# A two-layer kernel gets its tokens already transposed: the first norm moves into the weights and into the residual

## The reference, cut to what matters

```python
def _layernorm(x, axis=-1, eps=1e-05):
    m = jnp.mean(x, axis=axis, keepdims=True)
    v = jnp.var(x, axis=axis, keepdims=True)
    return (x - m) / jnp.sqrt(v + eps)
...
        w_masked = weight * elem_mask.astype(weight.dtype)     # blocks of 32 x 32, kept where the mask's sum is > 0
        out = jnp.einsum('bsk,nk->bsn', data, w_masked)
...
        logits = x @ W_gate + b_gate
        _, top_idx = jax.lax.top_k(logits, TOP_K)               # 2 of 8 experts
        y_all = jax.nn.relu(jnp.einsum('bsd,edh->bseh', x, W_e) + b_e)
        y = jnp.take_along_axis(y_all, top_idx[..., None], axis=2)
        return y.mean(axis=2)
    x = L0_attn_data                                            # 4 x 512 tokens of 1024 features, fp32
    x = x + _L0_attn_ref(_layernorm(x, axis=-1), L0_attn_weight, L0_attn_mask)
    x = x + _L0_ffn_ref(_layernorm(x, axis=-1), L0_ffn_W_gate, L0_ffn_b_gate, L0_ffn_W_e, L0_ffn_b_e)
```

## Time and profile before

| | |
|---|---|
| median of 3 runs | 734.63 us (734.1 to 734.97) |
| the profiled execution's own time | 734.0 us |
| its span, first to last instruction | 732.3 us |
| TensorE busy | 708.0 us, 97% |
| VectorE (DVE) busy | 332.2 us, 45% |
| ScalarE (ACT) busy | 238.9 us, 33% |
| GpSimd (POOL) busy | 290.5 us, 40% |
| mean granted TensorE clock | 0.996 |

### The profile page before, as it was taken

How to read it: one execution, slowest core, us unless ns; L and a number is a source line. 1 busy time by engine, 2 the same in 40 slices (tenths; PEclk the granted TensorE clock), 3 DMA queues, 4 the chain that set the end, 5 groups by cost and what they waited for, 6 DMA issues and landing times.

```text
span 732.3 us, 11399 instructions
## 1 busy us (share of the span) xinstructions
PE 708.0 (97%) x3655; PEld 579.1 (79%) x3655; DVE 332.2 (45%) x667; ACT 238.9 (33%) x316; POOL 290.5 (40%) x302
## 2 busy tenths in 40 slices
PE   3999999999999999999999999999999999999994
PEld 2468888888777878888888888888888888888883
DVE  4756777778899665635254261062342540000000
ACT  2231311311532232433342324333332323333320
POOL 5612112112453315563545445363544445353430
PEclk9999999999999999999999999999999999999998
DMA  8723443447563437868669486487686674331313
GB/s 318 286 86 116 166 159 136 172 146 288 208 224 115 145 144 195 243 156 259 154 173 245 107 235 162 91 213 218 132 256 157 174 197 81 66 59 29 58 30 57
DMA packets 34502, 118.22 MB, mean 161 GB/s; under 512 B 5776, under 2 KB 5776, under 8 KB 34448
## 3 DMA queue, kind: packets, MB, share of 16 engines
q1 hardware_dynamic: 22032, 80.23, 30.3%
q0 software_dynamic: 11232, 37.23, 25.2%
q10 hardware_dynamic: 1184, 0.04, 0.1%
HBM read 83.40 MB, written 37.75 MB: 165 GB/s over the span
## 4 chain that ended last, share of the span: by engine, by line
PE 91%; DVE 5%; issue 2%; DMA 1%; ACT 0%; POOLq 0%; SPq 0%; DVEq 0%
PE psO L316 78%; PE psT L420 5%; PE psT L351 2%; PE psG L455 2%; PE psT L343 1%; PE psO L382 1%; DMA xb<-L_attn_data 1%; PE psS L382 1%; DVE row_hot L739 1%; DVE st L654 1%; PE psT L438 1%; DVE pos_i L730 1%; DVE xr L681 1%; DVE blk_hot L737 0%; PE psG L330 0%
## 5 line engine op out<-in xcount | busy, mean ns | idle before, releaser
L316 PE MATMUL psO<-slots,xT 128*128 (+1 forms) x1872 | 436.0, 392 | 0.0
L316 PEld LDWEIGHTS psO<-slots,xT 128*128 128x128 f32 x1872 | 348.3, 188 | 70.6
L316 PE MATMUL psO<-wT,xT 128*128 128x512 f32 x768 | 184.1, 395 | 0.0
L316 PEld LDWEIGHTS psO<-wT,xT 128*128 128x128 f32 x768 | 141.5, 188 | 29.8 <-issue 0.9
L1055 POOL DMA_INDIRECT rows_out<-xb,tok_of x37 | 62.8, 1697 | 222.5 <-ACT xb L622 216.3
L807 DVE CAST slots<-raw 128x1024 fp32r<-128x1024 f32 x56 | 57.1, 1020 | 192.5 <-PE psO L316 109.0
L622 ACT ACTIVATE xb<-psO 128x512 f32<-128x512 f32 x78 | 46.7, 599 | 253.7 <-PE psO L316 253.7
L1049 POOL TENSOR_TENSOR xT<-x2T,xT 128x1024 fp32r<-128x1024 f32 x38 | 99.7, 2624 | 18.5 <-ACT x2T L601 18.1
L809 DVE TENSOR_TENSOR slots<-raw,slots 128x1024 fp32r<-128x1024 f32 x56 | 72.8, 1299 | 1.9
L533 ACT ACTIVATE xT<-psT 128x1024 fp32r<-128x1024 f32 x17 | 17.5, 1027 | 147.1 <-PE psT L351 136.6
L564 ACT ACTIVATE psO<-bias_slot 128x512 f32 (+1 forms) x78 | 47.0, 602 | 36.3 <-ACT xb L622 18.6
(11 more groups left out here) (160 smaller groups left out, 467.7 us busy)
## 6 DMA issues: line engine op xcount, KB each, us to landing
raw<-L_ffn_W_e SPq DMA_DIRECT2D x56, 512.0 KB, 5.2
xb<-L_attn_data SPq DMA_DIRECT2D x16, 512.0 KB, 3.4
xr<-L_attn_data SPq DMA_DIRECT2D x16, 512.0 KB, 4.1
rows_out<-xr SPq DMA_DIRECT2D x16, 512.0 KB, 2.7
x_rows<-x SPq DMA_DIRECT2D x16, 512.0 KB, 2.9
mask_stage<-L_attn_mask SPq DMA_DIRECT2D x8, 512.0 KB, 11.6
w_stage<-L_attn_weight SPq DMA_DIRECT2D x8, 512.0 KB, 12.3
bias_slot<-L_ffn_b_e SPq DMA_DIRECT2D x8, 512.0 KB
```

Of the source, the lines that this page charges most:

```text
L316: last = eng.matmul(psum, xT[:, p, a, kt, :], moving(b, kt), start=(i == 0 and kt == 0 and not seeded), stop=(i == len(PASSES) - 1 and kt ...
```

## The change

The host also hands over the tokens with each 128x128 square transposed (`data_t`), so `xb` holds raw transposed tokens, and `transpose_x`, `norm1` and the matmuls and ACT passes that they cost go. ACT and DVE read the two parts from `xb` in SBUF instead of from PSUM. The mean of a token is taken off by taking the row mean off each row of the masked weight (`centre`, on ACT; the mean comes from a summing ACT pass for even r, from a summing DVE multiply for odd r, so POOL multiplies only even r). 1/std multiplies the product in the residual. `stats1` reads `xr` instead of `xb`, and stands one block ahead at the end of a step instead of two blocks ahead near its start. SP loads `xb` when `x_lo` has read its half, not when TensorE has. 16 and 56 small fp16 matmuls on constants (`warm`) stand on each side of the first `group_sums`. `group_sums(r + 1)` stands ahead of `transpose_w(r)` instead of two row blocks ahead behind the fold.

```diff
-        ST, TOP, HOT, RS1, RS2 = 3, 12, 8, 5, 4
+        ST, TOP, HOT, RS1, RS2 = 3, 12, 8, 2, 4
...
+        X0_AT = 3
+        WARM = (16, 56)
...
             def load_x(t):
                 if t >= 2:
-                    eng.wait_ge(c_t1, t - 1)
-                eng.dma_start(xb[:, t % 2, :], data[t * P:(t + 1) * P, :]).then_inc(l_x[t % 2], 16)
+                    eng.wait_ge(c_xlo, t - 1)
+                eng.dma_start(xb[:, t % 2, :], data_t[t]).then_inc(l_x[t % 2], 16)
...
             def transpose_w(r):
                 eng.wait_ge(c_wm, r + 1)
 
-                if r == 2:
-                    eng.wait_ge(c_xlo, 1)
-                else:
-                    before = 1 if r == 1 else r - 1
-                    if before > 0:
-                        eng.wait_ge(c_whi, before)
-                        eng.wait_ge(c_wlo, before)
+                if r >= 2:
+                    eng.wait_ge(c_whi, r - 1)
+                    eng.wait_ge(c_wlo, r - 1)
...
+            def warm(n):
+                for _ in range(n):
+                    eng.matmul(psT[:, 1, 0, :], ones16[:], tri[:], start=True, stop=True)
+
             eng.wait_ge(s_const, NCONST)
+            warm(WARM[0])
             group_sums(0)
-            group_sums(1)
+            warm(WARM[1])
             for r in range(NT):
+                if r + 1 < NT:
+                    group_sums(r + 1)
                 transpose_w(r)
...
-            eng.wait_ge(c_wlo, NT - 1)
-            transpose_x(1)
             eng.wait_ge(c_fold_out, 1)
...
                     project_half(i, 0)
-                if 2 <= i + 1 < NB:
-                    transpose_x(i + 1)
...
+            def centre(r):
+
+                eng.wait_ge(c_masked[r % 2], r // 2 + 1)
+                if r % 2 == 0:
+                    if r > 0:
+                        eng.wait_ge(c_mean[0], r // 2)
+                    eng.activation(x2T[:].rearrange("p k t -> p (k t)"), w_stage[:, r, :], ACT.Copy, scale=-1.0 / D,
+                                   accum_out=minus_mean[:, r:r + 1]).then_inc(c_mean[0], 1)
+                eng.wait_ge(c_mean[r % 2], r // 2 + 1)
+                eng.activation(w_stage[:, r, :], w_stage[:, r, :], ACT.Identity,
+                               bias=minus_mean[:, r:r + 1]).then_inc(c_wm, 1)
...
+            for r in range(NT):
+                centre(r)
+                if r > 0:
+                    w_hi(r - 1)
+                if r == X0_AT:
+                    x_hi(0)
+            w_hi(NT - 1)
...
-                if i + 2 < NB:
-                    norm1(i + 2)
...
             def stats1(t):
-                eng.wait_ge(l_x[t % 2], 16 * (t // 2 + 1))
+                eng.wait_ge(l_xr[t % 2], 16 * (t // 2 + 1))
...
-                eng.tensor_tensor(xr[:, t % 2, cols], xr[:, t % 2, cols], psO[:, n, :], ALU.add).then_inc(c_res, 1)
+                eng.scalar_tensor_tensor(xr[:, t % 2, cols], psO[:, n, :], kept[:, t:t + 1], xr[:, t % 2, cols],
+                                         ALU.mult, ALU.add).then_inc(c_res, 1)
...
+            def masked_and_mean(r):
+
+                eng.wait_ge(c_em, r + 1)
+                eng.wait_ge(s_w[r], 16)
+                rows = w_stage[:, r, :].rearrange("p (g s) -> p g s", s=SUB)
+                eng.scalar_tensor_tensor(rows, rows, 1.0, emask[:, r, :].unsqueeze(2).to_broadcast([P, NSUB, SUB]),
+                                         ALU.mult, ALU.mult, accum_out=w_sum[:, r:r + 1]).then_inc(c_masked[1], 1)
+                eng.wait_ge(c_masked[1], r // 2 + 1)
+                eng.tensor_scalar(minus_mean[:, r:r + 1], w_sum[:, r:r + 1], -1.0 / D, None, ALU.mult).then_inc(c_mean[1], 1)
...
+                if r % 2 == 1:
+                    masked_and_mean(r)
+                if r >= 2:
+                    w_lo(r - 2)
+                if r == X0_AT:
+                    x_lo(0)
...
-                if i + 2 < NB:
-                    stats1(i + 2)
                 if i >= 1:
                     top2(i - 1)
...
+                if i + 1 < NB:
+                    stats1(i + 1)
```

More of the change, by code:

```diff
@@ L19, with build @@
 PASSES = [(HI, HI), (HI, LO), (LO, HI)]
-def build(nc, data, weight, mask, w_gate, b_gate, w_e, b_e, out):
+def build(nc, data, weight, mask, w_gate, b_gate, w_e, b_e, data_t, out):
     N_TOK, D = data.shape
@@ L529, in x_hi, with w_hi @@
             def x_hi(t):
-                eng.wait_ge(c_t1, t + 1)
+                if t == NB:
+                    eng.wait_ge(c_t1, 1)
+                else:
+                    eng.wait_ge(l_x[t % 2], 16 * (t // 2 + 1))
                 if t >= 2:
                     eng.wait_ge(c_mm, NH * (t - 1))
[L533 to L542, removed]
+                eng.activation(xT[:, t % 2, HI, :, :], x_side(t), ACT.Copy).then_inc(c_xhi, 1)
+            def centre(r):
[8 more added lines that the diff above has]
+                               bias=minus_mean[:, r:r + 1]).then_inc(c_wm, 1)
+            def w_hi(r):
                 eng.wait_ge(c_wt, r + 1)
                 eng.activation(wT[:, HI, :, r * P:(r + 1) * P], psT[:, w_half_of(r), :, :], ACT.Copy).then_inc(c_whi, 1)
-                if r == 0:
+            for r in range(NT):
[3 more added lines that the diff above has]
+                if r == X0_AT:
                     x_hi(0)
-                if r == X1_AT:
-                    norm1(1)
+            w_hi(NT - 1)
             eng.wait_ge(c_fold, 1)
@@ L832, in _ @@
             for r in range(NT):
-                for t in range(2):
-                    if r == t * X1_AT:
-                        stats1(t)
+                if r > 0:
+                    element_mask(r)
+                if r % 2 == 1:
+                    masked_and_mean(r)
+                if r >= 2:
+                    w_lo(r - 2)
+                if r == X0_AT:
+                    x_lo(0)
+                if r == 2:
+                    eng.wait_ge(s_small, 32)
+                    eng.tensor_reduce(wg_part[:], wg[:].rearrange("p k e -> p e k"), AX.X, ALU.add).then_inc(c_part, 1)
                 if r + 1 < NT:
                     sum_mask(r + 1)
[L838 to L849, removed]
             w_lo(NT - 2)
@@ L1019, in gather_rows @@
                                        bounds_check=known - 1, oob_is_err=False).then_inc(l_gather[b % 4], 16)
-            for r in range(NT):
+            for r in range(0, NT, 2):
                 eng.wait_ge(c_em, r + 1)
```

73 lines of the change are left out of this document (31 added, 42 removed).

## The result

The changed kernel takes **747.97 us** (median of 4 runs, 746.93 to 750.47) against 734.8 (734.1 to 735.04) for the one before in the same session: ratio 1.0186, 95% interval 1.016 to 1.0212. The prediction said slower, 736.6, and its range ended at 741.5: right in sign, 11 us short in size. The profiled execution took 746.93 us, its span is 745.2 (before 732.3).

What follows compares the result with a forecast made beforehand. TensorE, busy 97% of the span, was taken as the bound, with a 13.3 us ring through DVE and SP setting the changed steps. Start +5.0 and first layer -3.0 gave +2.0: 736.6 us, range 729.5 to 741.5.

Steps and rivals of the forecast that it cites:

- The start: Before the first step's logits: row blocks 0, 2, 3, 4 and the end give -2.3, +1.7, +3.7, +1.6, +0.3, together +5.0 us.
- the 1.6 us: Row block 4 of the start: its own POOL, mean and centring chain ends after block 3's fold, +1.6 us.
- the clock falls in the gap: Start, block 3: clock falls to 1.2 GHz in 4 us without work; 738.2 us, 17% shared with the multiply rival.
- Its other half: Start, odd rows: DVE's summing multiply at half speed, 2.4 us instead of 1.4; 738.2 us, within the same 17%.
- The ring: First-layer steps: residual, x_lo, SP, xr, stats1, next residual take 13.3 us, longer than TensorE's 12.8.
- `xr` lands 5.5 to 6.3 us after the issue; I take 5.95: First-layer steps: landing time of xr counted from the issue of xb, putting it at r + 11.8.
- a pair from the start, 4.9 us: Two transfers issued 0.37 us apart ended 4.9 us after the first issue; one more adds 1.0 to 1.4.
- Steps 8 and later: First layer: step 8 takes 14.6 us, step 9 15.8, steps 10 to 12 13.8 each, then 10.2 + 12.8 + 13.7.
- transfers slower: Rival, 8%, first-layer steps: xr lands 6.8 us after the issue, seven steps at 14.15, +6.0, 742.6 us.
- the heavy step: Step 9 of the first layer: bias and two weight chunks go ahead; xr alone took 7.4 us to land.
- The short ring: Rival, 25%, first layer: xr lands within 5.3 us, so a step is at most TensorE's 12.8; -4.3, 730.3 us.

Runs made afterwards that it cites:

- Experiment 2: The changed kernel with SP's order xb, xr, second norm's store, so one transfer stands ahead of xr instead of two: 737.07 us.
- experiment 1: The changed kernel with the load of xr put first on SP's queue, no longer waiting behind x_lo, and xb last: 726.06 us.
- experiment 6: experiment 1 with sum_mask(r+1) ahead of DVE's copies, and 18 and 48 small constant matmuls ahead of transposes 2 and 4: 724.33 us.
- experiment 3: The changed kernel with sum_mask(r+1) ahead of the copies of row block r on DVE: 750.21 us.
- experiment 7: experiment 6 without its 18 and 48 filling matmuls: 725.92 us.

## Why the prediction was wrong

**The start: right.** +4.6 against +5.0. The four places came where they were put: transposes at 12.40 (forecast 12.65), block 2 at 20.27 (20.5), `group_sums(4)` at 26.47, released by `sum_mask(4)`, and the transposes of block 3 at 26.91 (27.3), of block 4 at 31.74 (31.9). But at block 4 the split was other than said: of the 1.6 us only 0.22 is a wait, the rest is block 3 run slowly. The rival "the clock falls in the gap" came true and cost next to nothing extra, since block 4 would have waited anyway for its centred rows. Its other half did not: DVE's summing multiply, L840, takes 1.23 us and 0.08 for reading the sum:

```profile
19.03 1.23 DVE L840 SCALAR_TENSOR_TENSOR w_stage<-w_stage,emask 128x1024 f32<-128x1024 f32 x1
...
20.18 0.08 DVE L840 DVE_READ_ACCUMULATOR w_stage<-w_stage,emask 128x1 f32 x1
```

The Trainium skill (Vector Engine (DVE) Microarchitecture Reference, Points that are easy to get wrong) has this form with two SBUF sources that aren't bf16 at half throughput, 2.3 us by my estimate; the measurement disagrees, and it decides.

**The ring: the right mechanism.** First residual 2.68 us behind the logits (forecast 2.75), and DVE idle ahead of `stats1` and released by the DMA to `xr`: as written. `positions` were released by `chosen` in five of the seven steps, not from the first on: in step 1 and in step 3, behind the slow half product at 80.23, TensorE came later than `chosen`.

**The step that failed is "`xr` lands 5.5 to 6.3 us after the issue; I take 5.95".** Over steps 1 to 7 `xr` landed 7.57, 7.04, 6.76, 6.66, 6.74, 8.43 and 6.65 us after the issue of `xb`, 7.12 on average, and `x_lo` ended at r + 6.04, not 5.85. That gives 14.63 a step and not 13.3, +9.3 us in seven steps, some 8 of them from the landing and 1.3 from `x_lo`. The term that was mis-sized is the base of the sum: I took a pair from the start, 4.9 us, with nothing issued behind it, and added one transfer of 1.0 to 1.4, for which I had no row. Experiment 2 has such a pair inside a step, with a store issued right behind, and there it needs 5.96 on average; the second transfer ahead then adds 1.2 on average (0.7 to 2.5), about what was taken. Why the pair is slower there stays open. Being inside a step doesn't do it by itself: in the kernel before, a store and the load of `xr` issued 0.42 us behind it, with a load of `xb` 2.2 us ahead and nothing right behind, had both landed 4.2 to 4.6 us after the store's issue in steps 1 to 7. That points to the third transfer, but no run changes only that.

**Steps 8 and later: nearly right.** Between residuals step 8 took 14.65 (14.6), step 9 15.40 (15.8), steps 10 to 12 together 43.57 (41.4), the rest 37.14 (36.7). The sum of the first layer: 215.8 against 204.4, of which 9.3 is the seven ring steps and 2.2 steps 10 to 12. Those 2.2 are the same cause: `stats1` waited 0.18, 1.77 and 0.20 us for `xr` there. In experiment 1, where it doesn't wait, these steps take 13.7 to 13.8 us, the forecast's 13.8. `x_lo` came about 0.9 us before POOL's splits and took its usual 1.22 us.

The rival "transfers slower" was the right one: its landing of 6.8 and step of 14.15 were still 0.3 and 0.5 short, and it had 8 in 100. The range stopped at 741.5 because the widest landing in the rows was never carried through the seven steps: at the heavy step's 7.4, counted from the issue of `xb`, the sum would have come to 736.6 + 7 x 1.45 = 746.8, and even that is 1.2 us short of the measured time.

**The short ring**, with 25 in 100, was forecast at 730.3. Experiment 1 opens the ring and gives 726.06: the 5.2 us of waits that it assumed in steps 8 to 12 were 2.5 (12.8, 12.8, 13.0, 13.8 and 14.1 us between logits). My reading is that `xr`, loaded early, gives DVE slack there.

## What to carry to other kernels

When an operand is taken from another buffer, follow that buffer's whole round: who frees it, which queue reloads it, and what is issued ahead of the reload. Here the taken-out transposes were worth 8 us only after the load that closes the ring was put first on its queue. Here a transfer's time depended on its neighbours in the queue: price such a load from a row with the same neighbours, and carry the worst landing seen, multiplied by the steps that repeat it, into the range. And a wait of some 3 us on TensorE cost more than itself here unless something else hid the slow stretch behind it; cheap matmuls on constants in the waits gave 1.9 us at the start, and nothing in the steps of the ring.

The best version that leaves nothing out is experiment 6, 724.33 us, 1.35% below the kernel before.

## What the runs showed of the hardware

- In steps 1 to 7, a 0.5 MB load of `xr` lands 4.0 to 4.6 us after its issue when issued first of three (experiment 1), 5.4 to 5.6 us when issued 0.4 us behind one other, with one behind it (experiment 2), and 5.4 to 7.5 us when issued 0.9 to 1.4 us behind the first of two (the changed kernel).
- ACT's summing pass takes 1.06 us and 0.19 for reading the sum; DVE's summing multiply of 128x1024 fp32 takes 1.23 and 0.08, where `x_lo`, of the same size and without a sum, takes 1.22.
- After waits of 2.6 to 3.3 us TensorE's transposes or fold behind them ran at about half speed, at one of two places: from the first transpose (1.81 us in experiment 3), or only from the fold on (1.70 and 1.91 in experiment 7), behind the same 2.82 us wait. After the 1.51 us wait at block 2 they ran at full speed. In the changed kernel's steps, the half product behind waits of 2.02, 2.93 and 2.41 us took 7.3 to 8.6 us, and behind waits of 0.2 to 1.6 us 5.7; in experiment 3 one wait of 2.38 us left it at 5.70.
